# Four pairs of relu blocks a quad added by accumulating DMAs in an attention and expert layer

## What is computed

```python
xn = layernorm(x)
# attention, 16 heads of depth 8
s = einsum('bhtd,bhsd->bhts', q, k)
s = s - s.mean(axis=-1, keepdims=True)
mad = abs(s).mean(axis=-1, keepdims=True) + 1e-06
s = s / mad * score_gain
s = where(causal, s, -1000.0)
r = maximum(s, 0.0) ** 4
att = r / (r.sum(axis=-1, keepdims=True) + 1e-06)
y = einsum('bhts,bhsd->bhtd', att, v)
# experts: 8, the best 2 for each token, a gated network with silu
out = x + proj(y) + sum_of_two_experts(xn)
```

## Times and profile before

| | |
|---|---|
| median of 3 runs | 893.3 us (892.43 to 896.93) |
| the profiled execution | 888.43 us |
| its span in the trace | 886.7 us |
| PE busy | 740.6 us, 84% |
| DVE busy | 724.4 us, 82% |
| ACT busy | 683.5 us, 77% |
| POOL busy | 623.9 us, 70% |
| mean granted TensorE clock | 0.942 of full speed |

### The profile page before, as it was taken

The page is one execution under the profiler, slowest core; times in us unless marked ns, Lnnn a source line. Parts: engine busy times, 40 slices in busy tenths (PEclk is TensorE's granted clock), DMA queues, the critical chain, the costliest instruction groups (busy, mean ns, idle before and its releaser), DMA issues.

```text
span 886.7 us, 17644 instructions
## 1 busy us (share of the span) xinstructions
PE 740.6 (84%) x5719; PEld 335.2 (38%) x5719; DVE 724.4 (82%) x2043; ACT 683.5 (77%) x1639; POOL 623.9 (70%) x545
## 2 busy tenths in 40 slices
PE   0572888888999999899898989989999999989872
PEld 0530222222444454444344344444434444443222
DVE  7689898989777978786876977787787977778896
ACT  0573888888987878898886787888888887878870
POOL 5262777884897687686876776787777777778773
PEclk9995797979998999999999899999999999999895
DMA  8449703155325304250523423252323605230703
GB/s 270 136 190 264 307 32 85 43 156 156 59 83 167 114 18 131 84 129 19 141 85 59 146 72 70 90 141 85 58 91 99 179 11 141 82 57 10 215 6 101
DMA packets 60330, 97.10 MB, mean 110 GB/s; under 512 B 7360, under 2 KB 39744, under 8 KB 60240
## 3 DMA queue, kind: packets, MB, share of 16 engines
q1 hardware_dynamic: 54544, 86.22, 34.1%
q0 software_dynamic: 4544, 9.38, 3.3%
q10 hardware_dynamic: 1152, 0.40, 0.2%
HBM read 61.29 MB, written 34.36 MB: 108 GB/s over the span
## 4 chain that ended last, share of the span: by engine, by line
PE 45%; DVE 23%; ACT 13%; issue 12%; POOL 4%; DMA 1%; DVEq 1%; SPq 0%; ACTq 0%; POOLq 0%
PE bank L859 19%; DVE W L1177 10%; PE bank L894 7%; ACT U L788 7%; PE bank L874 6%; DVE junk_V L1169 5%; PE bank L914 4%; PE bank L899 3%; ACT W L799 3%; PE bank L921 2%; ACT junk_A L780 2%; POOL W L660 1%; POOL W L669 1%; DVE zT L1127 1%; POOL sorted_x L610 1%
## 5 line engine op out<-in xcount | busy, mean ns | idle before, releaser
L1177 DVE SCALAR_TENSOR_TENSOR W<-bank,U 128x512 f32<-128x512 f32 (+3 forms) x768 | 373.8, 549 | 40.1 <-ACT U L788 38.0
L788 ACT ACTIVATE U<-bank 128x512 f32<-128x512 f32 (+3 forms) x768 | 318.5, 519 | 48.3 <-PE bank L921 35.3
L859 PE MATMUL bank<-W,VS 128*10 128x512 f32 (+3 forms) x1536 | 297.8, 507 | 13.5 <-ACT yq L772 7.2
L859 PE MATMUL bank<-U,usel 128*10 128x512 f32 (+3 forms) x1536 | 292.7, 507 | 0.0
L1169 DVE TENSOR_SCALAR_CACHE_REDUCE junk_V<-bank 128x512 bf16<-128x512 f32 (+3 forms) x445 | 218.3, 533 | 88.2 <-PE bank L914 87.5
L669 POOL TENSOR_TENSOR W<-W 128x1024 f32<-128x1024 f32 (+2 forms) x159 | 231.6, 1460 | 53.9 <-DVE W L1177 45.9
L660 POOL TENSOR_TENSOR W<-W,causal 128x512 f32<-128x512 f32 x128 | 163.6, 1278 | 108.5 <-DVE W L1177 106.9
L799 ACT ACTIVATE W<-W 128x256 f32<-128x256 f32 (+2 forms) x225 | 191.6, 880 | 10.4 <-POOL W L660 10.2
L921 PE MATMUL bank<-QS,KS 48*128 48x512 bf16 (+3 forms) x768 | 162.9, 337 | 39.3 <-DVE W L1177 17.3
L780 ACT ACTIVATE junk_A<-bank 128x512 bf16<-128x512 f32 (+3 forms) x195 | 87.7, 460 | 57.2 <-PE bank L914 56.8
L914 PE MATMUL bank<-KS,QS 48*128 48x512 bf16 (+3 forms) x640 | 102.0, 328 | 17.0 <-DVE junk_V L1169 8.5
(11 more groups left out here) (158 smaller groups left out, 604.5 us busy)
## 6 DMA issues: line engine op xcount, KB each, us to landing
wb<-in_experts SPq DMA_DIRECT2D x39, 707.0 KB
qk_stacked<-parts SPq DMA_DIRECT2D x8, 768.0 KB, 11.7
QS<-qk_stacked SPq DMA_DIRECT2D x32, 192.0 KB
KS<-qk_stacked SPq DMA_DIRECT2D x32, 192.0 KB
xt_all<-sorted_x SPq DMA_DIRECT2D x39, 130.0 KB, 6.0
qk_stacked<-parts SPq DMA_DIRECT2D x8, 512.0 KB, 11.7
gat<-weighted_y SPq DMA_DIRECT2D x8, 512.0 KB, 6.6
sorted_x<-xt_all SPq DMA_DIRECT2D x3, 1300.0 KB, 11.7
```

The lines of the kernel that those rows point to most:

```text
L788: act.activation(U[n % NU][:, g, 0:w], score(4 * n + g)[:, 0:w], ACT.Relu).then_inc(u_ready, 1)
L859: last = pe.matmul(acc[32 * g:32 * g + VW, lo:HALF], usel[:, :] if of_u else VS[q % 2][:, j, g, :], (U if of_u else W)[n % NU][:, g, 0:HAL ...
L1177: vec.scalar_tensor_tensor(W[n % NU][:, g, 0:w], score(4 * n + g)[:, 0:w], 0.0, U[n % NU][:, g, 0:w], ALU.max, ALU.mult).then_inc(w_done, 1)
```

## The change

Four pairs of units a quad are formed: (0, 1), (4, 5), (6, 7), (8, 9). The first of a pair is called "to", the second "from". When both U are written, POOL issues a DMA that adds U of the second to U of the first, where they lie in SBUF (for (0, 1) and (8, 9) shifted by 128 columns, since the second is narrower). PE then multiplies no U when it averages a unit of a pair, only W; two iterations after the average of the first (`ADDLAG`) it waits for the DMA and multiplies the sum by `usel`, behind that iteration's other averaging matmuls. The other units (2, 3, 10, 11) keep their own U matmuls. The DMAs count on two semaphores in turn.

U gets a fifth slot; W keeps four (`NW`). ACT waits, before it writes a slot that held the first of a pair, for the average two units later, and before one that held the second, for the DMA that read it.

POOL's DMA stands in its queue in iteration n of the second unit, after the expert scatters and before the mask and squares of n, behind waits for W of unit n - 1 and U of unit n.

```diff
-    NU, AVLAG = 4, 2
+    NU, NW, AVLAG, ADDLAG = 5, 4, 2, 2
+    ADD_TO = [0, 4, 6, 8]
+    ADDS = [n for n in range(ALL) if n % NS in ADD_TO]
+    is_to, is_from = (lambda n: n % NS in ADD_TO), (lambda n: (n - 1) % NS in ADD_TO)
+    added = lambda n: (ADDS.index(n) % 2, 16 * (ADDS.index(n) // 2 + 1))
...
         U = [tmp(f"U{i}", [P, 4, HALF]) for i in range(NU)]
-        W = [tmp(f"W{i}", [P, 4, HALF]) for i in range(NU)]
+        W = [tmp(f"W{i}", [P, 4, HALF]) for i in range(NW)]
...
-                slot, w = W[n % NU], HALF - LOW[n % NS]
+                if is_from(n):
+                    (par, _), off = added(n - 1), LOW[n % NS] - LOW[(n - 1) % NS]
+                    pool.wait_ge(w_done, 4 * n)
+                    pool.wait_ge(u_ready, 4 * (n + 1))
+                    pool.dma_start(U[(n - 1) % NU][:, :, off:HALF - LOW[(n - 1) % NS]], U[n % NU][:, :, 0:HALF - LOW[n % NS]],
+                                   accum_op=ALU.add).then_inc(u_added[par], 16)
+                slot, w = W[n % NW], HALF - LOW[n % NS]
...
-                    w = HALF - LOW[n % NS]
-                    wait(act, used, n - NU + 1)
+                    w, old = HALF - LOW[n % NS], n - NU
+                    wait(act, used, old + 1 + ADDLAG * (old >= 0 and is_to(old)))
+                    if old >= 0 and is_from(old):
+                        par, count = added(old - 1)
+                        act.wait_ge(u_added[par], count)
...
-                    average(y, 0, False)
-                    average(y, 1, True)
-                    average(y, 0, True)
-                    average(y, 1, False).then_inc(used, 1)
+                    average(y, 0, False, first=first)
+                    if is_to(y) or is_from(y):
+                        last = average(y, 1, False, first=first)
+                        if y >= ADDLAG and is_to(y - ADDLAG):
+                            pe.wait_ge(u_added[added(y - ADDLAG)[0]], added(y - ADDLAG)[1])
+                            for p in range(2):
+                                last = average(y - ADDLAG, p, True)
+                    else:
+                        average(y, 1, True, first=first)
+                        average(y, 0, True, last_of=end)
+                        last = average(y, 1, False, last_of=end)
+                        if y >= ADDLAG and is_to(y - ADDLAG):
+                            pe.wait_ge(u_added[added(y - ADDLAG)[0]], added(y - ADDLAG)[1])
+                            for p in range(2):
+                                last = average(y - ADDLAG, p, True)
+                    last.then_inc(used, 1)
...
-                wait(vec, used, n - NU + 1)
+                wait(vec, used, n - NW + 1)
```

More of the change, by code:

```diff
@@ L247, in layer_kernel @@
         s_ready, u_ready, w_done, w_mask = sem("scores_ready"), sem("u_ready"), sem("w_done"), sem("w_masked")
-        r_ready = [sem(f"r_ready{i}") for i in range(NU)]
+        r_ready = [sem(f"r_ready{i}") for i in range(NW)]
         used = sem("u_and_r_used")
+        u_added = [sem("u_added0"), sem("u_added1")]
         acc_ev = sem("acc_evacuated")
@@ L797, in _ @@
                             act.wait_ge(w_done, 4 * y + 2 * p + 2)
-                        some = W[y % NU][:, 2 * p:2 * p + 2, 0:HALF - LOW[y % NS]]
-                        act.activation(some, some, ACT.Square).then_inc(r_ready[y % NU], 1)
+                        some = W[y % NW][:, 2 * p:2 * p + 2, 0:HALF - LOW[y % NS]]
+                        act.activation(some, some, ACT.Square).then_inc(r_ready[y % NW], 1)
         @block.tensor
@@ L852, in _, with average @@
                 k_and_q(b)
-            def average(n, p, of_u):
+            def average(n, p, of_u, first=False, last_of=False):
                 q, (c, j), lo = n // NS, STEPS[n % NS], LOW[n % NS]
@@ L860, in average @@
                                      usel[:, :] if of_u else VS[q % 2][:, j, g, :],
-                                     (U if of_u else W)[n % NU][:, g, 0:HALF - lo],
-                                     start=(j == 0 and of_u == bool(p)), stop=(n % NS in ENDS and of_u != bool(p)),
-                                     skip_group_check=True)
+                                     U[n % NU][:, g, 0:HALF - lo] if of_u else W[n % NW][:, g, 0:HALF - lo],
+                                     start=first, stop=last_of, skip_group_check=True)
                 return last
@@ L940, in _ @@
                 if y >= 0:
-                    pe.wait_ge(r_ready[y % NU], 2 * (y // NU + 1))
-                    if STEPS[y % NS][1] == 0:
+                    pe.wait_ge(r_ready[y % NW], 2 * (y // NW + 1))
+                    first, end = STEPS[y % NS][1] == 0, y % NS in ENDS
+                    if first:
                         wait(pe, acc_ev, y // NS * CH + STEPS[y % NS][0])
-                    average(y, 0, False)
-                    average(y, 1, True)
-                    average(y, 0, True)
-                    average(y, 1, False).then_inc(used, 1)
+                    average(y, 0, False, first=first)
[14 more added lines that the diff above has]
+                    last.then_inc(used, 1)
             for e in "VA":
```

6 lines of the change are left out of this document (3 added, 3 removed).

## The result

| | before | after |
|---|---|---|
| median, first chip | 892.87 us | 928.12 us (926.66 to 933.46) |
| the profiled execution | 888.43 us | 933.46 us |
| mean granted TensorE clock | 0.942 | 0.880 |

The ratio is 1.0396, 95% interval 1.0343 to 1.0449: the change makes the kernel 35 us slower, where 23 us less were forecast. The two profiled executions are 45 us apart, more than the medians, and what is read from their traces shares that. Lines have moved: L873 is the average (L859 before), L927 pieces (L914), L934 scores (L921), L671 the mask (L660), L680 POOL's squares (L669), L813 ACT's squares (L799), L666 the adding DMA.

The account below looks back on a forecast made before the run. PE's averaging matmuls were taken to bound 13 of 16 quads. 3.2 us per quad, less 0.4 for masks and 1.0 for waits, left 1.8, or 23 us over 13 quads: 870 us from 893.3, range 852 to 915.

Parts of the forecast that it names:

- 3.2 us a quad: PE's saving at best from the dropped U matmuls, counted in the 13 quads that PE bounds.
- a discount of 1.0: Per quad, 1.0 us off PE's gain because four engines at 84 to 90% make PE wait for them more often.
- the two gains fall on iterations 4 and 0, where the chain doesn't run through PE: The moved sums add 0.84 us of PE work to each of these iterations, where PE was not taken to bound.
- less 0.4 for the masks of units 1 and 9: On POOL, masks queued behind the added DMAs delay ACT's square; 0.4 us per quad was deducted.
- it just holds: POOL's square of unit 4 slips from 594.37 to 596.9 us, still before PE wants it at 597.2.
- both are hidden with 3 to 5 us to spare: Sums (4,5) and (0,1) land in 6.0 and 5.6 us, within windows of 11 and 8.5 us.
- the late rival: DMA reads and writes one after the other, large sums land after 13.4 us, PE stalls: about 950 us; chance 0.18.
- where only some sums are late: The milder case of the rival in which sums land after PE asks for them: 900 us.
- I cost their delay at nothing: Loads of expert weights and the next quad's data, issued iterations ahead, lose 0 us to the added DMA traffic.
- POOL's issue, the rival at 893 us: Issuing 512 pieces costs POOL 4.1 us, some 3 us per quad against 3.2 won: 886 to 902 us; chance 0.2.
- The granted clock: Sign of being wrong in another way: a granted clock below the 1.00 of the quad studied.

Follow-up runs that it names:

- shorter list: The changed kernel without its 64 accumulating DMAs and the waits on them, against the kernel before on the same chip: 880.7 us, ratio 0.9721.
- issue: The kernel without DMAs, given 64 DMAs of as many pieces but 16 bytes each, PE not waiting for them: 903.53 us, ratio 0.9952 to the kernel before.
- bytes: The changed kernel with whole DMAs, PE multiplying the second unit's U and waiting for no DMA: 913.41 us, ratio 1.0100 to the kernel before.
- waits for sums: The full change, PE waiting for sums, rerun on another chip against the kernel before: 930.53 us, ratio 1.0252; without PE's waits the ratio was 1.0100.
- copied bytes: The changed kernel without PE's waits, SP issuing plain copies of the same bytes in place of POOL's DMAs: 892.74 us, ratio 0.9838 to the kernel before.

## Why the prediction was wrong

The change on these chips in one line, each term a difference of two neighbouring kernels: shorter list -25, issue +21, bytes +13, waits for sums +14: +23 us. Each is good to some 3 to 7 us by its interval. Issue and bytes were measured against each other across chips; their sum of 34 us was measured on one.

**PE's gain: right in size, wrong in its parts.** The forecast had 3.2 us a quad less a discount of 1.0, 2.2 over 13 quads or 29 us; measured are 2.0 and 25. The step that failed is "the two gains fall on iterations 4 and 0, where the chain doesn't run through PE": they cost 0.56 and 0.54 of the 0.84 us put there. Iterations 6 and 7, for which 1.1 to 1.3 us had been expected, gave 0.58. The chain of one quad had been taken for all quads.

**Issue: the price right, its effect more than three times too small.** 1.0 and 1.5 us were forecast, 0.95 and 1.43 measured. The step that failed is "less 0.4 for the masks of units 1 and 9", and the "it just holds" ahead of it. A mask behind a DMA ends 2.74 us after the start of the DMA (0.86 + 1.88), not 1.27: it is held for the whole issue. The 21 us are 1.3 us for each of 16 quads, and by the traces 1.8 us for each of quads 3 to 14. The argument about the square of unit 4, "it just holds", did not hold either: issues ahead of squares cost 6.8 us over these twelve quads, as much as those ahead of masks. By which waits the rest of the 21 us comes about was not shown.

**Landing: the step "both are hidden with 3 to 5 us to spare" failed.** 6.0 and 5.6 us were forecast, 8.6 and 7.8 are the medians, and the spread, for which there was no term, did the harm: 6.7 to 13.7 us. Worked out from the trace, PE found 14 of the 64 sums missing, with landings of 8.8 to 13.7 us. The windows had been forecast well enough: PE asked for the late (6, 7) some 11 us after its issue, as forecast. The transfer rate was one cause (182 GB/s, not 285). The other, worked out from the same trace and not tested by a run of its own, is the traffic beside them, which the long landings go with. The SP queue moved under 0.1 MB during the landing of 31 of the sums, and these took 6.7 to 8.8 us (medians 7.1 large, 6.9 small). It moved 1 MB or more during that of 16, and these took 8.6 to 13.7 (medians 10.0 and 11.0). Counted over a fixed stretch, from 3 us before the issue to 7 us behind it, the third of the sums with the most of this traffic has 15 of the 16 landings over 9.5 us. It is the late rival in a milder form: that one wanted 13.4 us for every large sum. What it foresaw "where only some sums are late" is what happened, at 14 us.

**Traffic: "I cost their delay at nothing" failed.** 13 us, of which the waits for expert weights (4.6 us in that kernel, 4.9 in the change) and up to 3.6 us of ACT's added waits are the parts that can be named. The rest is spread over waits that no row names. And the late sums are the other side of the same traffic.

**POOL's issue, the rival at 893 us,** had the wrong cause (512 pieces cost 1.4 us, not 4.1) and the right balance for the issue alone, no gain (0.9952), from a smaller gain and a smaller loss than its 3 us a quad. It was a rival of its own; the result is what comes of it, late sums and traffic at once. The chances treated them as alternatives, and left 0.05 to anything else. A single term left the change a gain or level where it was measured: 0.9952 with the issue, 0.9838 with copied bytes.

**The granted clock** was named as a way to be wrong. It fell from 0.942 to 0.880 on the first chip, in the early quads above all (0.70 against 0.86 in 150 to 200 us). There it costs little: from 100 to 240 us the kernel with the shorter list has 0.77, the kernel before, on another of these chips, 0.87 (rows below, the first the shorter list), and their first three quads take 142.7 and 144.2 us.

```profile
100.00:240.00 140.00, 114.34 (x746) 31.88 (x743) 120.93 (x370) 114.42 (x223) 92.72 (x88) 0.77 0.33 98
```

```profile
100.00:240.00 140.00, 115.94 (x834) 33.29 (x835) 120.98 (x375) 113.41 (x225) 91.68 (x88) 0.87 0.33 97
```

From 240 to 850 us it fell from 0.97 to 0.94. There the clock falls behind stalls of PE's, as at 595.58 and 624.40. How much of the 14 us is the waiting and how much the slow matmuls behind it was not separated and stays open.

## What to carry to other kernels

Work taken off the bounding engine must be charged, instruction by instruction, for what its replacement puts in front of the steps that other engines wait for: two issues a quad of 1.4 us ahead of masks cost 1.8%; two of 0.95 us ahead of squares cost as much in twelve of the quads and looked free (0.2%) only because the first three happened to get shorter. A transfer that is hidden by its median time is not hidden; compare the window with its longest time, beside the loads that run at the same time. And where four engines stand near 80%, several small costs are not rivals but terms of one sum.

## What the runs showed of the hardware

- A DMA that adds in SBUF moved 182 GB/s over its queue's busy time, a plain copy of the same bytes 377.
- Landing of 1024 KB sums took 8.6 us in the median and up to 12.4, that of 768 KB sums in 512 pieces 7.8 and up to 13.7. With next to nothing on the other queue they took 6.7 to 8.8 us, beside 1 MB or more of it 8.6 to 13.7.
- POOL's issue of a DMA took 0.95 us for 128 pieces and 1.4 for 512, whether a piece was 8 or 1.5 KB or 16 bytes. The row of the instruction behind it starts within it and is longer (a mask 1.88 us instead of 1.27); together they take the issue and the usual mask.
- PE's matmuls ran at half speed behind stalls of 1.5 and 3.1 us, at a granted clock of 0.52 and 0.50: the x8 group of 1.04 us took 1.90. Behind another stall of 3.1 us it took 1.05.
- The kernel before differed by 1.4 to 1.8% between chips (892.9 and 905.8 to 909.2), the kernel after by 0.3%.
